# Rotary attention: single projection of four heads with transfers, scaling shared by two engines

## The reference, cut to what matters

```python
def _rope(x, theta):
    angles = jnp.arange(seq)[:, None] * theta
    cos, sin = jnp.cos(angles)[None, None], jnp.sin(angles)[None, None]
    x1, x2 = (x[..., 0::2], x[..., 1::2])
    return jnp.concatenate([x1 * cos - x2 * sin, x1 * sin + x2 * cos], axis=-1)

xn = _rmsnorm(x, gamma1)
q = _rope(heads(xn @ q_w + q_b), theta)      # 16 heads of 64
k = _rope(heads(xn @ k_w + k_b), theta)
v = heads(xn @ v_w + v_b)
attn = softmax(causal(q @ k.T / 8))
attn_out = (attn @ v) @ o_w + o_b + xn
an = _rmsnorm(attn_out, gamma2)
```

## Time and profile before

| | us |
|---|---|
| median of 3 runs (1768.97 to 1774.07) | 1769.36 |
| the profiled execution | 1769.51 |
| its span, first to last instruction | 1767.5 |
| busy in the span: TensorE | 1551.0 (88%) |
| vector engine | 1113.3 (63%) |
| ScalarE | 931.6 (53%) |
| Pool | 555.9 (31%) |
| rotary stage, first projection to last instruction | 1107 to 1499 |

### The profile page before, as it was taken

How to read it: one execution, slowest core, us unless ns; L and a number is a source line. 1 busy time by engine, 2 the same in 40 slices (tenths; PEclk the granted TensorE clock), 3 DMA queues, 4 the chain that set the end, 5 groups by cost and what they waited for, 6 DMA issues and landing times. The chain is left out here.

```text
span 1767.5 us, 29904 instructions
## 1 busy us (share of the span) xinstructions
PE 1551.0 (88%) x11045; PEld 847.0 (48%) x11045; DVE 1113.3 (63%) x2537; ACT 931.6 (53%) x2028; POOL 555.9 (31%) x690
## 2 busy tenths in 40 slices
PE   1677686699999999999999997899999997599999
PEld 1344343244454444454545443566666675244444
DVE  4755442477878686878787783566566654355554
ACT  1323233176777777776777676355555554243343
POOL 4010101121121203030303000688788885133331
PEclk9978787599999999999999999999999999699998
DMA  4222210703233323223132220000000000000001
GB/s 101 70 55 55 55 37 18 141 16 98 48 98 48 99 48 99 48 88 57 70 56 62 61 33 6 4 1 1 1 1 1 1 1 1 10 20 20 22 19 37
DMA packets 88422, 75.35 MB, mean 43 GB/s; under 512 B 24725, under 2 KB 78389, under 8 KB 87349
## 3 DMA queue, kind: packets, MB, share of 16 engines
q1 hardware_dynamic: 88276, 73.44, 18.9%
HBM read 42.73 MB, written 30.42 MB: 41 GB/s over the span
## 5 line engine op out<-in xcount | busy, mean ns | idle before, releaser
L1145 DVE TENSOR_REDUCE b_chunk_max<-psum 128x1 f32<-128x400 f32 (+1 forms) x1024 | 540.9, 569 | 176.7 <-PE psum L1359 170.6
L1283 ACT ACTIVATE b_prob<-psum 128x512 f32<-128x512 f32 (+1 forms) x832 | 451.2, 594 | 180.7 <-PE psum L1398 178.9
L1359 PE MATMUL psum<-k_stack,q_stack 128*128 128x400 bf16 (+1 forms) x1024 | 285.4, 343 | 21.0 <-DMA k_stack<-b_k_scratch 17.9
L1368 PE MATMUL psum<-b_prob,b_v_aug 128*32 128x256 f32 (+1 forms) x3328 | 265.9, 391 | 1.7 <-ACT b_prob L1283 0.4
L1398 PE MATMUL psum<-q_stack,k_stack 128*128 128x256 bf16 (+1 forms) x1664 | 253.0, 275 | 0.4 <-DMA q_stack<-b_mparts 0.4
L1398 PEld LDWEIGHTS psum<-q_stack,k_stack 128*128 128x128 bf16 (+1 forms) x1664 | 146.3, 99 | 117.9 <-ACT b_prob L1283 68.8
L1557 POOL TENSOR_SCALAR c_prob<-c_prob,c_rec 128x128 f32<-128x128 f32 (+1 forms) x256 | 191.9, 767 | 8.9 <-POOL c_kT L1566 8.3
L2036 DVE TENSOR_TENSOR e_hg<-e_gl,e_gate 128x512 f32<-128x512 f32 x128 | 123.3, 979 | 113.2 <-PE psum L2051 75.5
L1640 DVE SCALAR_TENSOR_TENSOR c_turned<-psum,c_bias,c_tab 128x256 f32<-128x256 f32 x256 | 106.1, 476 | 112.0 <-PE psum L1773 112.0
L1675 ACT ACTIVATE c_prob<-psum,c_mneg 128x128 f32<-128x128 f32 (+1 forms) x256 | 104.1, 419 | 136.7 <-DVE c_mneg L1617 136.7
L1359 PEld LDWEIGHTS psum<-k_stack,q_stack 128*128 128x128 bf16 x1024 | 99.7, 98 | 128.6 <-DVE b_chunk_max L1145 95.5
(11 more groups left out here) (213 smaller groups left out, 1971.0 us busy)
## 6 DMA issues: line engine op xcount, KB each, us to landing
k_stack<-b_k_scratch SPq DMA_DIRECT2D x32, 600.4 KB, 10.5
b_k_scratch<-b_kparts SPq DMA_DIRECT2D x7, 1200.8 KB, 4.4
b_k_scratch<-b_kparts SPq DMA_DIRECT2D x7, 800.5 KB, 6.3
b_ctx<-in_ctx SPq DMA_DIRECT2D x8, 576.0 KB
e_w<-in_L_ffn_re_w SPq DMA_DIRECT2D x62, 64.0 KB, 1.8
a_scratch<-a_parts SPq DMA_DIRECT2D x16, 192.0 KB, 2.2
k_stack<-a_scratch SPq DMA_DIRECT2D x16, 192.0 KB, 4.7
q_stack<-b_q_scratch SPq DMA_DIRECT2D x32, 96.0 KB, 2.2
```

The source lines that it names most:

```text
L1145: nc.vector.tensor_reduce(out=chunk_max[:, half, q, column4(hh), c:c + 1], in_=max_bank(v)[:, 0:w], axis=AX.X, op=ALU.max).then_inc(max_do ...
L1283: nc.scalar.activation(prob[0:k, buf, par * 2 * T:(par + 1) * 2 * T], st_bank(v, par)[0:k, :], ACT.Exp, scale=HD ** -0.5).then_inc(exp_don ...
L1359: nc.tensor.matmul(max_bank(T_.now("unit"))[:, 0:hi - lo], queries_of(qst, h, slice(q * P, q * P + P)), keys_of(kst, h, slice(lo, hi)), st ...
L1368: last = nc.tensor.matmul(pv[32 * hh:32 * hh + 32, :], v_aug[0:k, kt, g * GH + hh, :], prob[0:k, buf, c:c + T], start=(kt == 0), stop=(kt ...
```

## The change: what it does

Before the launch, the columns of the q and k weights and biases are reordered on the host, so that one 128-column block holds the even elements of four heads (two units) and the next block the odd ones. One slot now projects either q (even slots) or k (odd slots) for four heads with two matmuls in place of four. The vector engine makes four products from the two halves with sine and cosine. Pool makes `second` (one sum) and the first halves (a difference, written for both units), and SP moves the second halves to their partitions with four transfers of 32 rows a slot, 256 in all. The scores wait for these transfers and move from lag 2 to lag 3. `NORM_LAG` is gone: the scaling goes with the turn's lag, 4. The vector engine scales the first query tile of each head (128 columns), Pool the second (256 columns). The vector engine's order in a slot becomes: reciprocal and narrow scalings, maximum, rotation products, norm stage, output sum. TensorE's becomes: value item, scores, projection, output product, value products, turn. Pool's keeps power or residual first, then scaling, then sums. At the start the weight ordering on Pool, 14 of the small transfers and one sign change of the table fall away.

```diff
-SCORES_LAG, NORM_LAG, TURN_LAG, VALUES_LAG = 2, 3, 4, 5
+SCORES_LAG, TURN_LAG, VALUES_LAG = 3, 4, 5
...
+            for n in range(B * UN):
+                m, u, buf = n % 2, n % UN // 2 * 2, n % 2
+                sp.wait_ge(turned_ready, n + 1)
+                for pos in range(4):
+                    to = 32 * (pos ^ 1)
+                    sp.dma_start((qT, kT)[m][to:to + 32, u + pos % 2, :], second[32 * pos:32 * pos + 32, buf, :])\
+                        .then_inc(placed[m], 16)
...
                 if ("o", 0) in c_items(n, first, drain):
                     power()
                 ahead()
-                w = c_unit(n, NORM_LAG, first, drain)
+                w = c_unit(n, TURN_LAG, first, drain)
                 if w is not None:
                     pool.wait_ge(rec_ready, T_.up("weigh"))
-                    pool.sem_inc(passed, 1)
                     for hh in range(2):
-                        for lo, hi, q in ((0, P, 0), (P, 3 * P, 1)):
-                            ins = nc.gpsimd.tensor_scalar(prob[:, w % PB, hh, lo:hi], prob[:, w % PB, hh, lo:hi],
-                                                          rec[:, w % PB, hh, q:q + 1], None, ALU.mult)
-                    ins.then_inc(weighed, 1)
+                        ins = nc.gpsimd.tensor_scalar(prob[:, w % PB, hh, P:3 * P], prob[:, w % PB, hh, P:3 * P],
+                                                      rec[:, w % PB, hh, 1:2], None, ALU.mult)
+                    ins.then_inc(wide_weighed, 1)
                 if u is not None:
-                    pool.wait_ge(terms_ready, T_.up("unit"))
-                    par = u % 2
-                    nc.gpsimd.tensor_tensor(qT[:, u, :], turned[:, par, 0, 0, :], turned[:, par, 0, 1, :], ALU.add)\
-                        .then_inc(own_pool, 1)
+                    v = T_.up("unit")
+                    pool.wait_ge(terms_ready, v)
+                    m, g, t4 = u % 2, u // 2 * 2, terms[:, u % 2]
+                    if v > UN:
+
+                        pool.wait_ge(s_full, (v - 1) // 2 * 2 + 2 - UN)
+                    if v > 2:
+
+                        pool.wait_ge(placed[m], 64 * ((v - 1) // 2))
+                    nc.gpsimd.tensor_tensor(second[:, m, :], t4[:, 2, :], t4[:, 3, :], ALU.add).then_inc(own_pool, 1)
                     pool.wait_ge(own_pool, T_.up("own_pool"))
-                    nc.gpsimd.tensor_tensor(kT[:, u, :], turned[:, par, 1, 0, :], turned[:, par, 1, 1, :], ALU.add)\
-                        .then_inc(turned_ready, 1)
-                    pool.wait_ge(turned_ready, T_.now("unit"))
+                    for j in range(2):
+                        nc.gpsimd.tensor_tensor((qT, kT)[m][:, g + j, :], t4[:, 0, :], t4[:, 1, :], ALU.subtract)\
+                            .then_inc((own_pool, turned_ready)[j], 1)
+                        if j == 0:
+                            pool.wait_ge(own_pool, T_.up("own_pool"))
+                    pool.wait_ge(turned_ready, v)
...
+                u = c_unit(n, TURN_LAG, first, drain)
+                if u is not None:
+                    dve.wait_ge(exp_done, T_.up("weigh"))
+                    nc.vector.reciprocal(rec[:, u % PB].rearrange("p h q -> p (h q)"),
+                                         total[:, u % PB].rearrange("p h q -> p (h q)")).then_inc(rec_ready, 1)
+                    dve.wait_ge(rec_ready, T_.now("weigh"))
+                    for hh in range(2):
+                        ins = nc.vector.tensor_scalar(prob[:, u % PB, hh, 0:P], prob[:, u % PB, hh, 0:P],
+                                                      rec[:, u % PB, hh, 0:1], None, ALU.mult)
+                    ins.then_inc(weighed, 1)
                 u = c_unit(n, SCORES_LAG, first, drain)
                 if u is not None:
                     dve.wait_ge(s_full, T_.up("scores"))
@@ -1616,11 +1623,18 @@
                     nc.vector.tensor_reduce(out=mneg[:, par, 0, :], in_=psum[:, 2:4, 0:P], axis=AX.X, op=ALU.max, negate=True)
                     nc.vector.tensor_reduce(out=mneg[:, par, 1, :], in_=psum[:, 2:4, P:3 * P], axis=AX.X, op=ALU.max, negate=True)\
                         .then_inc(m_ready, 1)
-                u = c_unit(n, NORM_LAG, first, drain)
+                u = c_unit(n, 0, first, drain)
                 if u is not None:
-                    dve.wait_ge(exp_done, T_.up("weigh"))
-                    nc.vector.reciprocal(rec[:, u % PB].rearrange("p h q -> p (h q)"), total[:, u % PB].rearrange("p h q -> p (h q)"))\
-                        .then_inc(rec_ready, 1)
+                    v = T_.up("unit")
+                    dve.wait_ge(proj_full, v)
+
+                    wait(dve, turned_ready, T_.now("unit", 2))
+                    m, bank = u % 2, (q_bank, k_bank)[u % 2]
+                    for dst, (half, wave) in enumerate(((0, 0), (1, 1), (0, 1), (1, 0))):
+                        ins = nc.vector.scalar_tensor_tensor(out=terms[:, m, dst, :], in0=bank[:, half * T:(half + 1) * T],
+                                                             scalar=bias[:, m, u // 2, half:half + 1], in1=tab[:, m, wave, :],
+                                                             op0=ALU.add, op1=ALU.mult)
+                    ins.then_inc(terms_ready, 1)
                 ahead()
                 items = c_items(n, first, drain)
                 if ("o", 0) in items:
@@ -1629,19 +1643,6 @@
                     finish(B - 1 if drain else i)
                 for it in items:
                     item(*it, None)
-                u = c_unit(n, 0, first, drain)
-                if u is not None:
-                    v = T_.up("unit")
-                    dve.wait_ge(proj_full, v)
-
-                    wait(dve, turned_ready, T_.now("unit", 2))
-                    for m, bank in enumerate((q_bank, k_bank)):
-                        for w in range(2):
-                            ins = nc.vector.scalar_tensor_tensor(out=turned[:, u % 2, m, w, :], in0=bank[:, w * T:(w + 1) * T],
-                                                                 scalar=bias[:, m, w, u:u + 1], in1=tab[:, m, w, :],
-                                                                 op0=ALU.add, op1=ALU.mult)
-                    ins.then_inc(terms_ready, 1)
...
-                    pe.wait_ge(turned_ready, T_.up("scores"))
+                    quads = (T_.up("scores") + 1) // 2
+                    pe.wait_ge(placed[0], 64 * quads)
+                    pe.wait_ge(placed[1], 64 * quads)
                     wait(pe, exp_done, T_.now("scores", 1))
...
                     last.then_inc(s_full, 1)
+                u = c_unit(n, 0, first, drain)
+                if u is not None:
+                    T_.up("unit")
+                    if n == 0:
+
+                        pe.wait_ge(item_free, T_.now("item"))
+                    wait(pe, terms_ready, T_.now("unit", 2))
+                    bank = (q_bank, k_bank)[u % 2]
+                    for half in range(2):
+                        last = nc.tensor.matmul(bank[:, half * T:(half + 1) * T], qkw[:, u % 2, u // 2, half, :], xT[:],
+                                                start=True, stop=True)
+                    last.then_inc(proj_full, 1)
                 if ("o", 0) in items:
 
                     pe.wait_ge(att_ready, T_.now("values"))
@@ -1755,24 +1770,13 @@
                 u = c_unit(n, TURN_LAG, first, drain)
                 if u is not None:
                     pe.wait_ge(weighed, T_.up("turn"))
+                    pe.wait_ge(wide_weighed, T_.now("turn"))
                     wait(pe, probT_ready, T_.now("turn", 1))
                     for hh in range(2):
                         for k in range(3):
                             last = nc.tensor.transpose(psum[:, 4 + hh, k * P:(k + 1) * P], prob[:, u % PB, hh, k * P:(k + 1) * P],
                                                        t["ident"][:])
                     last.then_inc(tp_full, 1)
-                u = c_unit(n, 0, first, drain)
-                if u is not None:
-                    T_.up("unit")
-                    if n == 0:
-
-                        pe.wait_ge(item_free, T_.now("item"))
-                    wait(pe, terms_ready, T_.now("unit", 1))
-                    for m, bank in enumerate((q_bank, k_bank)):
-                        for w, weights in enumerate((w1, w2)):
-                            last = nc.tensor.matmul(bank[:, w * T:(w + 1) * T], weights[:, m, u * P:(u + 1) * P], xT[:],
-                                                    start=True, stop=True)
-                    last.then_inc(proj_full, 1)
...
+        if name in ("L0_ffn_q_w", "L0_ffn_k_w"):
+            v = v.reshape(D, 4, 2, 2, 32, 2).transpose(0, 1, 5, 3, 2, 4).reshape(D, CH * CD)
+        if name in ("L0_ffn_q_b", "L0_ffn_k_b"):
+            v = v.reshape(4, 2, 2, 32, 2).transpose(2, 1, 3, 0, 4).reshape(P, UN)
```

(45 more changed lines are left out.)

7 lines of the change are left out of this document (2 added, 5 removed).

## The result

The changed kernel takes 1914.42 us (median of 4 runs, 1910.64 to 1921.61) against 1769.16 (median of four runs of the kernel before beside it): a ratio of 1.082, interval 1.0797 to 1.0847, so it is slower by 145 us. Predicted were 1893, range 1835 to 1935. The profiled execution took 1910.64 us, span 1908.8, mean granted clock 0.893 (before 0.937).

What follows compares the result with a forecast made beforehand. TensorE was taken as the bound, Pool second. Six middle batches growing from 47.26 to 66.7 us give +116.6, ends and prologue +6.7, together +123 on 1769.5: 1893 us, range 1835 to 1935.

Steps and rivals of the forecast that it cites:

- The chain: Slots with a norm: scores, maximum, rotation products, norm, power, two wide scalings, turn in sequence; slots of 8.3 to 12.5 us.
- Slots 4 and 0: Scores there wait for the key transfers of slots 3 and 7; slots last 5.6 and 6.15 us.
- The clock: TensorE runs slowly after four stalls a batch; 0 to 6.2 us lost, 4.5 taken, giving a batch of 66.7.
- The first batch: No scaling in slots 1 to 3, powers only delay unit 3's keys: about 36 against 39.7 us, -4.
- The drain: After the last batch: three score slots instead of two, +3.4 us.
- The prologue: Weight ordering on Pool, 5.57 us, falls away but ran beside the vector engine's split: 0 to 2 us, -1 taken.
- The narrow scalings at nothing: Vector engine's 16 a batch cost 0 of at most 3.2 us; 19 us more by the port rule for every one.
- Transfers: Four issued serially on SP take 4.0 us; projection to scores takes 10.3 us for two slots.
- B: Rival: TensorE's program is the pace and the stalls close, 1712 us; chance 0.05.
- E: Rival: the gain of 58 us and the stalls cancel, nothing measurable, 1770 us; chance 0.03.
- C: Rival: transfers are the pace, four larger ones needing 8 us instead of 4, +60, 1953 us; chance 0.07.
- D: Rival: only slots 2 and 5 stall fully, slots 1 and 3 by half, 1860 us at most; chance 0.13.

Runs made afterwards that it cites:

- with slack: Changed kernel with scaling at lag 4, turn at 5, values at 6, and Pool's power and residual last: 1783.34 us, 1.0073 of the kernel before.
- with ScalarE: Changed kernel with Pool's power and residual last and the two wide scalings on ScalarE instead of Pool: 1770.0 us, 0.9986 of the kernel before.

## Why the prediction was right, and where it fell short

**The number.** +123 us were forecast, the profiled execution is 141 us longer. Of the 18 us between them 8.7 lie in the six middle batches, 8.4 in the first and 4.9 in the drain; the last batch (-1.0) and the rest (-3.1) go the other way. The parts follow.

**The chain, right.** The turn in slot n needs the scaling of the same slot, and on Pool this stands behind the norm's power. Predicted and measured lengths of the slots, us, from the batch at 1214.08, and below them those of a batch in the kernel with filled stalls (from 1271.77), where the clock is 0.99 and so the forecast for full clock can be set against it:

| slot | 0 | 1 | 2 | 3 | 4 | 5 | 6 | 7 |
|---|---|---|---|---|---|---|---|---|
| predicted, full clock | 6.15 | 9.5 | 9.6 | 8.3 | 5.6 | 12.5 | 4.6 | 6.0 |
| measured | 6.09 | 10.61 | 10.47 | 10.56 | 5.34 | 13.79 | 5.23 | 6.21 |
| measured, stalls filled | 5.91 | 9.36 | 9.53 | 8.22 | 5.15 | 12.33 | 4.52 | 6.21 |

TensorE idles 4.75, 5.79, 4.40 and 4.15 us ahead of the turns of slots 1, 2, 3 and 5 (predicted 5, 6, 5 and 4). With the clock held, slots 1, 2, 3, 5, 6 and 7 come within about 0.2 us of the forecast. The cause is shown, not only argued: with power and residual behind the scaling and the sums, 134 us are gone, and everything else of the change is still there.

**Slots 4 and 0, right by luck.** Their forecast, 5.6 and 6.15 us, rests on scores that wait for transfers. In the changed kernel's middle batches no scores do: TensorE works through both slots with hardly a gap and is as late by its slow matmuls. With the clock held, slot 4 does end on a wait for transfers, of 0.85 us, and lasts 5.15:

```profile
1371.17 0.93 PE L1736 MATMUL psum<-c_kT,c_qT 64*128 64x128 f32 x8 [0.85 <-DMA c_kT<-c_second]
```

Slot 0 never does; there the turn waits for Pool's scaling, by 1.03 us.

**The sum at full clock, right.** 62.2 us a batch were predicted; with the clock held by dummy work it is 61.1.

**The clock, under-sized.** The row was weighed with the batches of the earlier trace rows whose mean stayed at 1.00, and 4.5 of at most 6.2 us were taken. Every stall was followed by slow work in every batch (0.80 to 0.82 in all six windows), at 1.2 of 2.4 GHz: 68.15 - 61.1 = 7.0 us a batch. The forecast counted four stalls. A fifth, of 1.83 us ahead of the turn in slot 7, is followed by slow work too, in the next slot 0:

```profile
1349.20 0.85 PE L1777 MATMUL psum<-ident,c_prob 128*128 128x128 f32 x6 [1.83 <-issue]
...
1352.39 1.91 PE L1750 MATMUL psum<-c_xT,c_w 128*128 128x256 f32 x4
```

The slow work also reaches further than counted. In slot 3 slow scores and a slow projection delay the maximum and the rotation, so that the exponential starts at S+3.3, not S+2.35, and the chain itself gets longer: 10.56 instead of 8.3. The chain came out 1.1 us shorter than forecast and the clock 2.5 us dearer, together 6 x (68.15 - 66.7) = 8.7 us.

**The first batch, wrong sign:** -4 predicted, +4.4 measured. The forecast left the transfers out here. The first scores wait 8.16 us for the first of them, behind projection, rotation and sums, with no other unit to work on, and the window's clock is 0.74:

```profile
1116.59 1.65 PE L1735 MATMUL psum<-c_kT,c_qT 64*128 64x128 f32 x8 [8.16 <-DMA c_kT<-c_second]
```

Without transfers the first batch takes 38.05 us, 6.1 less, and is shorter than before (39.71), as forecast in sign. That slot 4 has a turn, which waits 2.55 us, was left out too.

**The last batch, right:** +8.3 predicted, +7.3 measured. **The drain, under-sized:** +3.4 for one more score slot, +8.3 measured. The clock of 0.66 was left out; the output product takes 6.73 us instead of 3.84 in the drain before:

```profile
1628.15 6.73 PE L1714 MATMUL psum<-c_ow,c_attT 128*128 128x128 f32 x32 [0.57 <-ACT c_attT L1682]
```

In the kernel without transfers the drain's clock is 0.93 and the drain takes 29.2 us, +3.8, so one more score slot was priced about right.

**The prologue:** -1 predicted. The stage starts 4.6 us earlier, but no part of it can be put down to the removed ordering: the first mask product of self-attention comes at 59.06 instead of 60.02, but in the other kernels with this same prologue at 59.07 to 60.75, and the start of the rotary stage's x transposition varies between them from 1101.2 to 1107.2 us (before: 1105.8). The 4.6 us are within that scatter; the term of -1 is not shown.

**The narrow scalings at nothing, right in sum, for a wrong reason.** The line L1616 has min, median and max of 271, 302 and 776 ns, mean 389, so about 0.05 us over the 0.34 each. But Pool didn't stand still while they ran: in the trace an instruction of Pool was running during every one of the 128. What they took depended on which. Beside the power (L1523) it was 0.27 to 0.30 us, and when one started just behind Pool's `second` it was 0.78:

```profile
1257.39 0.73 POOL L1558 TENSOR_TENSOR c_second<-c_terms 128x256 f32<-128x256 f32 x1 [2.92 <-DVE c_terms L1634]
1257.43 0.78 DVE L1616 TENSOR_SCALAR c_prob<-c_prob,c_rec 128x128 f32<-128x128 f32 x1
```

The shared port pair that "SBUF — State Buffer" in the Trainium skill speaks of ("Who interferes with whom") agrees in kind with the second case: the scaling ends 0.1 us behind Pool's sum. The 0.34 us of L149, which the forecast called undisturbed, also ran beside Pool, beside its scaling (L1557), and the 0.43 to 0.88 us beside its rotation sums; so the earlier trace rows compare two kinds of Pool's work, not Pool at work and Pool idle. Two smaller slips: 0.6 us for the two scalings of the norm doesn't lie between twice 0.34 and twice 0.88 (0.59 was measured all the same), and the 19 us are for six narrow scalings a batch, not for all sixteen.

**Transfers, near in sum, for another split.** The page's list of issues gives each one's size and its median from issue to landing, 1.8 us, and the timeline of SP a set of four with 2.41 us:

```profile
c_kT<-c_second SPq DMA_DIRECT2D x128, 32.0 KB, 1.8
```

```profile
1242.03 2.41 SPq L1513 DMA_DIRECT2D c_qT<-c_second  x4
```

The 2.41 us include the fourth issue (0.6), from whose start its 1.8 us count: 2.41 - 0.6 + 1.8 = 3.6, against the 4.0 from the earlier trace rows.

**The rivals.** B (faster, turns don't wait) and E (no change) are excluded by 137 us of wait. C (transfers are the pace) is excluded by the kernel without transfers: -11 us. But it was not far: as soon as the order is mended, the path that ends in the transfers is the next bound (42.4 us of waits with slack, 41.2 us with ScalarE), and two of four transfers on a second queue make a batch 3.2 us shorter; the prediction had them only as a time above A. D (parts overlap) is excluded by slots 1 and 3, which stall fully.

**Where the expected gain is.** Half the projection, 56 to 61 us of TensorE, didn't arrive: each time one wait was removed, another stood behind it, the norm on Pool, the scaling in the same slot, the path over the transfers, the clock. The best of these versions is 7 us below the kernel before. That the rest of the gain can be had was not shown.

## What to carry to other kernels

Before a lag between two engines is shortened, list what stands ahead of the producer in its own program: here one power of 0.72 us, waiting for another engine's norm, stood ahead of the scaling and cost more than the halved projection gave. Work that others wait for goes first, work with slack last, and a gap in TensorE's work was charged twice here, by its length and by slow matmuls behind it (21 us and 7 us a batch). When one wait is removed, follow the same consumer to its next producer before counting the gain.

## What the runs showed of the hardware

- Stalls of 4 to 6 us of TensorE were followed by slow work each time: scores of up to 1.65 us instead of 0.93, a projection of up to 1.92 instead of 1.03, a value item of 1.91 instead of 1.02. Two of 1.83 and 1.94 us also were, and one of 1.35 us behind dummy matmuls was not (0.93). Fifteen dummy matmul calls a batch took 30 us off the kernel.
- An issue of a transfer took 0.51 us on Pool, 0.55 to 0.59 on SP, so a second queue halves the time of issue but costs Pool 1 us a slot.
- A scaling of 128x128 on the vector engine took 0.27 to 0.30 us beside Pool's power and 0.78 us when it started just behind Pool's sum of 128x256.
- Why the next stage starts later after the version in which Pool issues transfers (13.8 against 5.2 us of wait) was not settled.
